# Two-layer conditional kernel on one core: the first batch's loads, turns and splits put in another order

## The reference

```python
# layer 0: x + x W0^T + b0 + coeff[b] * x (2 mask[b] - 1)
output = jnp.einsum('bsi,oi->bso', hidden_states, W) + b
sign = (2 * mask - 1).astype(hidden_states.dtype)
diff = jnp.einsum('bsi,bio->bso', hidden_states, sign)
x = x + output + diff * coeff[:, None, None]
# layer 1: y + y W1^T + b1 + (y A^T) B^T, A and B gathered by ids[b]
result = jnp.einsum('bsd,od->bso', x, base_weight) + base_bias
h = jnp.einsum('bsd,brd->bsr', x, lora_A_w[adapter_ids])
x = x + result + jnp.einsum('bsr,bor->bso', h, lora_B_w[adapter_ids])
```

## Time and profile before

| | |
|---|---|
| median of three runs | 433.26 us |
| the profiled execution, its time | 435.75 us |
| its span | 434.1 us |
| TensorE busy | 409.7 us (94%) |
| VectorE, ScalarE, GpSimd busy | 287.1, 184.6, 24.0 us |
| mean granted clock of TensorE | 0.978 of full speed |
| HBM read, written | 51.39 MB, 8.39 MB |

### The profile page before, as it was taken

The page is one execution under the profiler, slowest core; times in us unless marked ns, Lnnn a source line. Parts: engine busy times, 40 slices in busy tenths (PEclk is TensorE's granted clock), DMA queues, the critical chain, the costliest instruction groups (busy, mean ns, idle before and its releaser), DMA issues.

```text
span 434.1 us, 5456 instructions
## 1 busy us (share of the span) xinstructions
PE 409.7 (94%) x2049; PEld 342.3 (79%) x2049; DVE 287.1 (66%) x336; ACT 184.6 (43%) x288; POOL 24.0 (6%) x47
## 2 busy tenths in 40 slices
PE   3579998978999999999999999999999999999996
PEld 3568886757888888888888888888888888888884
DVE  0475658676688666776588767776678667866512
ACT  2264555454334533363343434444245433453312
POOL 4325401000000000000000000000000000000000
PEclk9788999899999999999999999999999999999999
DMA  6996796416943399309931595319921894237002
GB/s 224 253 333 195 207 211 179 86 48 151 249 125 94 108 193 222 97 1 233 237 100 50 131 240 150 98 74 209 236 64 36 196 241 120 61 110 169 2 0 97
DMA packets 90845, 63.28 MB, mean 146 GB/s; under 512 B 3515, under 2 KB 84419, under 8 KB 90820
## 3 DMA queue, kind: packets, MB, share of 16 engines
q1 hardware_dynamic: 89588, 59.28, 55.3%
q0 software_dynamic: 1232, 3.67, 2.7%
HBM read 51.39 MB, written 8.39 MB: 138 GB/s over the span
## 4 chain that ended last, share of the span: by engine, by line
PE 88%; DVE 6%; ACT 2%; DMA 2%; issue 1%; SPq 1%; ACTq 0%; DVEq 0%
PE ps L625 27%; PE ps L627 13%; PE ps L652 13%; PE ps L651 13%; PE ps L653 13%; PE ps L635 3%; PE ps L611 3%; PE ps L663 2%; DMA cs<-in_condB_coeff_dram 2%; DVE wm L488 1%; DVE wlo L495 1%; ACT whi L350 1%; DVE w1lo L460 1%; DVE xhl L471 1%; DVE xt L465 0%
## 5 line engine op out<-in xcount | busy, mean ns | idle before, releaser
L625 PE MATMUL ps<-xhl,whi 128*128 128x512 f32 x512 | 187.8, 405 | 2.0 <-DVE wlo L495 1.2
L627 PE MATMUL ps<-xhl,wlo 128*128 128x256 f32 x512 | 145.1, 283 | 0.0
L495 DVE SCALAR_TENSOR_TENSOR wlo<-wm,cs_minus,whi 128x1024 fp32r<-128x1024 f32 x64 | 83.0, 1296 | 53.2 <-ACT whi L350 52.8
L625 PEld LDWEIGHTS ps<-xhl,whi 128*128 128x128 f32 x512 | 97.7, 191 | 25.1 <-DVE wlo L495 1.5
L350 ACT ACTIVATE whi<-wm,cs_minus 128x1024 fp32r<-128x1024 f32 x64 | 73.7, 1151 | 81.7 <-DVE wm L488 80.5
L651 PE MATMUL ps<-w1hi,yhl 128*128 128x512 f32 x256 | 102.0, 398 | 0.0
L652 PE MATMUL ps<-w1lo,yhl 128*128 128x512 f32 x256 | 100.7, 394 | 0.0
L653 PE MATMUL ps<-w1hi,yhl 128*128 128x512 f32 x256 | 100.5, 393 | 0.0
L627 PEld LDWEIGHTS ps<-xhl,wlo 128*128 128x128 f32 x512 | 98.1, 192 | 2.5
L488 DVE SCALAR_TENSOR_TENSOR wm<-wm,cs_twice,w0t 128x1024 f32<-128x1024 int32 x64 | 81.8, 1278 | 11.7 <-ACT w0t L331 11.5
L652 PEld LDWEIGHTS ps<-w1lo,yhl 128*128 128x128 f32 x256 | 48.5, 189 | 10.7
(11 more groups left out here) (50 smaller groups left out, 178.7 us busy)
## 6 DMA issues: line engine op xcount, KB each, us to landing
wm<-in_mask_Bx4096x_ik_dram SPq DMA_DIRECT2D x64, 512.0 KB, 5.8
out_dram<-zst SPq DMA_DIRECT2D x32, 256.0 KB, 2.5
xraw<-in_x_dram SPq DMA_DIRECT2D x28, 256.0 KB, 7.4
w1raw<-_L_cond_base_weight_dram SPq DMA_DIRECT2D x8, 512.0 KB, 6.5
bt<-bhl SPq DMA_DIRECT2D x48, 64.0 KB, 2.9
w0raw<-in_L_cond_W_dram POOLq DMA_DIRECT2D x5, 512.0 KB, 6.7
w0raw<-in_L_cond_W_dram SPq DMA_DIRECT2D x3, 512.0 KB, 9.2
xrows<-in_x_dram SPq DMA_DIRECT2D x2, 512.0 KB, 7.0
```

The source lines that it names most:

```text
L495: nc.vector.scalar_tensor_tensor(wlo[:, s, :, :], wm[:, n % MS, :].rearrange("p (k o) -> p k o", k=KT), cs_minus[:, b:b + 1], whi[:, s, :, ...
L625: nc.tensor.matmul(ps[:, bank, :], whi[:, s, k, :], xhl[:, b % 2, k, :], start=(k == 0), stop=False, skip_group_check=True)
L627: op = nc.tensor.matmul(ps[:, bank, 0:S], wlo[:, s, k, :], xhl[:, b % 2, k, 0:S], start=False, stop=(k == KT - 1), skip_group_check=True)
```

## The change

Only batch 0 (and, in later batches, which half of x is turned first) changes. TensorE's, ScalarE's, VectorE's, GpSimd's and Sync's lists all move:

- the units get other banks: two banks for turning, 5 and 7; layer 0's product of steps 0 to 7 uses bank 4 alone, later ones 5 and 4 in turn;
- w0's chunk n+1 (not n+2) is turned in step n, so the weights are made one step ahead in batch 0, and VectorE catches up to two steps in step 7;
- A is turned inside step 1, B in step 4 instead of step 6; `adapter_h(0)` moves into step 2;
- the next x is turned by VectorE in the fourth and seventh step (n = 3 and 6), second half first;
- w0's chunks 3 to 7 go to Sync's list; four small loads go to ScalarE's queue; GpSimd issues A in pieces of 2, 4 and 2 around its first additions, B in two pieces of 4, and it splits the bias (`b1hi`, `b1lo`) that ScalarE and VectorE split before.

```diff
-    Z0, L1B, HB, TB = 0, 4, 6, 7
-    units = [("w0", 0, 0, 0), ("w0", 0, 1, 1), ("x", 0, 0, 4), ("x", 0, 1, 5), ("x", 1, 0, 6), ("x", 1, 1, 7),
-             ("w0", 1, 0, 2), ("w0", 1, 1, 3), ("w0", 2, 0, 0), ("w0", 2, 1, 1),
-             ("a", 0, 0, 2), ("a", 0, 1, 3), ("w1", 0, 0, TB), ("w1", 0, 1, HB)]
+    Z0, L1B, HB, TB = 0, 4, 6, (5, 7)
+    units = [("w0", 0, 0, 0), ("w0", 0, 1, 1), ("x", 0, 0, 2), ("x", 1, 0, 3), ("x", 0, 1, 6), ("x", 1, 1, 7),
+             ("w0", 1, 0, 0), ("w0", 1, 1, 1), ("w1", 0, 0, 2), ("w1", 0, 1, 3)]
     for n in range(1, KT):
...
+        if n + 1 < KT:
+            units += [("w0", n + 1, h, TB[h]) for h in range(2)]
+        if n == 4:
+            units += [("b", 0, h, TB[h]) for h in range(2)]
+        for h in range(2):
+            units.append(("w1", n, h, TB[h]))
+            if n == 1:
+                units.append(("a", 0, h, TB[h]))
...
+    def l1_bank(n):
+        return L1B if n < KT else L1B + (n + 1) % 2
...
@@ sync
...
             load_w1(1)
+            load_w0(3)
             load_mask(3)
...
             for n in range(NS):
+                if n + 4 < KT:
+                    load_w0(n + 4)
...
+                if n == 1:
+                    load_x(1)
                 if n == 3:
                     move_bias()
-                if n == 7:
+                if n == 5:
                     load_bt(0)
@@ gpsimd
             pool.wait_ge(ident_set, 2)
+            pool.wait_ge(ids_in, 16)
+            load_a(range(0, 2))
             eye_w0(0)
-            load_a()
+            load_a(range(2, 6))
             eye_w0(1)
+            load_a(range(6, NB))
             eye_w1(0)
-            load_w0(3)
             eye_w0(2)
-            load_w0(4)
             eye_w1(1)
-            load_w0(5)
             eye_w0(3)
-            load_w0(6)
+            load_b(range(0, 4))
             eye_w0(4)
             eye_w1(2)
+            load_b(range(4, NB))
             eye_w0(5)
-            load_b()
-            load_w0(7)
+            pool.wait_ge(b1_in, 16)
+            nc.gpsimd.tensor_copy(b1hi[:, :], b1raw[:, :]).then_inc(bias_hi, 1)
+            pool.wait_ge(bias_hi, 1)
+            nc.gpsimd.tensor_tensor(b1lo[:, :], b1raw[:, :], b1hi[:, :].bitcast(F32), ALU.subtract).then_inc(bias_lo, 1)
             eye_w1(3)
-            eye_w0(6)
@@ scalar
...
+            act.dma_start(cs[:, :], coeff.rearrange("(e b) -> e b", e=1).to_broadcast([P, NB])).then_inc(coeff_in, 16)
+            act.dma_start(b0row[:, :], b0.rearrange("(c p) -> c p", p=P)).then_inc(b0_in, 16)
+            act.dma_start(id_row[:, :], ids.rearrange("(e b) -> e b", e=1)).then_inc(ids_in, 16)
+            act.dma_start(b1raw[:, :], b1.rearrange("(e o) -> e o", e=1)).then_inc(b1_in, 16)
...
+                if n == 7:
+                    rows_hi(1, 0)
+                    chunk_hi(8)
+                half_y(n)
+                if n < 7:
+                    chunk_hi(n + 1)
                 y_parts_hi(n)
+                for h in range(2):
+                    split_hi("w1", n, h)
+                    if n == 1:
+                        split_hi("a", 0, h)
+                if n == 7:
+                    chunk_hi(9)
@@ tensor, layer1
+                    if n == 0:
+                        pe.wait_ge(b0_moved, 1)
+                    elif n < KT:
+                        pe.wait_ge(y_made, n)
+                    else:
+                        pe.wait_ge(y_made, n - 1)
+                    if n == KT:
+                        pe.wait_ge(parts_lo, parted(number["w1", KT - 1, 0]))
+                    if c == 0 and b > 0:
+                        pe.wait_ge(x_lo, x_split(b, 0))
```

More of the change, by code:

```diff
@@ L249, in _ @@
                     load_bt(b)
-                if c == 2 and b + 1 < NB:
+                if c == 3 and 0 < b < NB - 1:
                     load_x(b + 1)
@@ L270, in eye_w1, with load_a @@
                 nc.gpsimd.tensor_tensor(diag, diag, ident[:, :], ALU.add).then_inc(w1_eyed, 1)
[L272 to L278, removed]
-                for e in range(NB):
+            def load_a(adapters):
+                for e in adapters:
                     name = pool.value_load(id_row[0:1, e:e + 1], min_val=0, max_val=NL - 1)
@@ L524, in _ @@
             make_w(0)
-            first_rows_lo(0, 0)
             chunk_lo(0)
-            first_rows_lo(0, 1)
-            first_rows_lo(1, 0)
-            first_rows_lo(1, 1)
-            dve.wait_ge(b0_turned, 1)
-            nc.vector.tensor_copy(b0col[:, :], ps[:, TB, 0:KT]).then_inc(b0_moved, 1)
+            for g in range(2):
+                for st in range(ST):
+                    first_rows_lo(st, g)
             make_w(1)
@@ L584, in turn_unit @@
                 before = [v for v in range(u) if units[v][3] == bank]
-                if u == number["w1", 0, 0]:
-                    pe.wait_ge(b0_moved, 1)
                 if before and units[before[-1]][0] == "x":
-                    pe.wait_ge(x_lo, 4)
+                    pe.wait_ge(x_lo, first_split(*units[before[-1]][1:3]))
                 elif before and units[before[-1]][0] == "w0":
@@ L615, in layer1 @@
                 b, c = divmod(n, KT)
-                bank = L1B + n % 2
+                bank = l1_bank(n)
                 s = n % WS
@@ L703, in _ @@
                     pe.wait_ge(consts_set, 3)
-                    pe.wait_ge(w0_copied, copied(number["w0", 2, 1]))
+                    pe.wait_ge(w0_copied, copied(number["w0", 1, 1]))
+                    pe.wait_ge(parts_lo, parted(number["w1", 0, 1]))
+                    pe.wait_ge(y_lo, 1)
+                    layer2(0, 0, 0)
+                    turn_unit("w1", 1, 0)
+                    layer2(0, 0, 1)
+                    turn_unit("a", 0, 0)
+                    layer2(0, 1, 0)
+                    turn_unit("w1", 1, 1)
+                    turn_unit("a", 0, 1)
+                    layer2(0, 1, 1)
+                    continue
                 if m < KT:
```

180 lines of the change are left out of this document (84 added, 96 removed).

## The result

The changed kernel takes **442.54 us** (median of four runs, 441.93 to 443.49), the kernel before 433.44 us beside it on the same chip: a ratio of **1.020, 95% interval 1.014 to 1.026**. It is slower, by some 9 us (whether by more than 2% the interval leaves open), where 435.5 us (431.0 to 439.5) was forecast.

A forecast was written before the change was run, and what follows sets the result against it. TensorE, busy without a gap from 100.60 us, bounds the kernel, so only step 9's start can move: +0.55 us, plus 1.7 for half clock, gives +2.25 on the median of 433.26, so 435.5 us, range 431.0 to 439.5.

The forecast's parts named there:

- Start: Up to step 1: numbers land in 3.0 us, first addition at 8.3, step 1 at 25.8 against 27.60, gain 1.8 us.
- A in step 1: TensorE waits 2.5 and 1.7 us before A's two halves; step 2 at 38.1 against 40.18, 0.4 for half clock.
- Steps 2 to 4: TensorE waits for GpSimd's additions to w1's chunks 2 and 3, done at 44.35 and 53.25; step 5 at 65.7.
- Steps 5 to 9: End of batch 0: step 7 at 81.7, step 8 at 90.65 held by VectorE, step 9 at 101.15.
- The wait before `finish`: In step 8, TensorE waits 3.7 us for VectorE's chain where 1.78 stood before.
- the 1.7 us that I added for it: Behind step 9: half clock after the last wait adds 1.7 us, half of 3.4.
- The sum: Step 9 later by 0.55 us plus 1.7 for half clock: +2.25 us, profiled execution 438.0, median 435.5.
- (A): Whole kernel: the sum holds, all waits from the lists' order and measured durations, 435.5 us, slower; chance 0.38.
- (B): Step 0, step 2 and last wait: TensorE's clock does not fall, 432.6 us, no change; chance 0.2.
- (C): Steps 3 and 4: GpSimd not late, B loads at 0.55 us each, 432.1, or 430.5 with (B) in part; chance 0.2.
- (D): Numbers land at 7.2, b1lo takes 3.6, or half clock follows the wait before step 1: 437 to 440; chance 0.22.

The follow-up runs named there:

- e5: Changed kernel with the four small loads issued from Sync's queue again, ids first, coefficients behind x: 442.30 us, ratio 1.0205.
- e4: Changed kernel with GpSimd's descriptor space at 1536 bytes instead of 1024, h's parts put over `abraw`: 437.69 us, ratio 1.0104.
- e10: Changed kernel with e3's order, A in bank 6, batch 0's end reordered, bias and w1 chunk 2's addition earlier, descriptor space 1024 bytes: 432.84 us, ratio 0.997.
- e1: Changed kernel with GpSimd's addition to w1's chunk 3 moved ahead of the second piece of B loads: 438.49 us, ratio 1.0107.
- e3: Changed kernel with the addition to w0's chunk 0 again ahead of all A loads: 440.72 us, ratio 1.0168.
- e12: e10 with descriptor space of 1536 bytes, h's parts over `abraw`, and w1 chunk 3's addition ahead of b1hi: 424.25 us, ratio 0.978.

## Why the prediction was right or wrong

Starts of the steps, as forecast and as measured:

| step | 0 | 1 | 2 | 3 | 4 | 5 | 7 | 8 | 9 |
|---|---|---|---|---|---|---|---|---|---|
| forecast | 16.5 | 25.8 | 38.1 | 47.7 | **56.2** | 65.7 | 81.7 | 90.65 | 101.15 |
| measured | 17.38 | 25.81 | 38.27 | 47.00 | **62.53** | 71.73 | 87.83 | 96.82 | 107.13 |

- **Start: right by luck.** The addition came at 8.97 (forecast 8.3; its terms add to 8.2), and step 1 at 25.81 as forecast, but only because two errors of 0.9, in step 0's start (17.38 for 16.5) and in its length (8.43 for 9.3), cancel. The numbers took 7.29 - 1.5 - 1.91 = 3.9 us to land (1.5 is the prediction's time from a number to its first load; GpSimd's read of `id_row` starts at 5.7), against the 3.0 taken; first in Sync's own queue (e5) they took 3.67 - 1.5 - 0.86 = 1.3. By the Trainium skill (DMA: Bandwidth & Descriptors, section Queues, rings and completion order) each DMA engine takes its queue rows in turn. The prediction's estimate of 2 us from that rule was too low for the numbers behind two other loads on ScalarE's queue.
- **A in step 1: right.** Waits of 2.5 and 1.7 were forecast, 2.31 and 1.41 came. Half clock behind them, taken at 0.4 us, did not come in this execution (1.00 from 36 to 48 us); in e4's and e5's it did (0.76 and 0.72), and step 2 started there at 39.75 and 40.85.
- **Steps 2 to 4: this step failed.** "Next, four more loads, an addition, b1hi, b1lo, then the addition to w1's chunk 3: ... 8.9, done at 53.25." It was done at 56.80, 12.9 after the one to chunk 2 (43.88). Of the 4.0 more, 3.3 are the pause before the eighth load (e4, e10), 0.8 is b1lo: 3.20 for 2.4, inside its bounds of 1.2 to 3.6. The prediction had no term for a pause. Nor had it one for the clock here: behind the 5.16 us wait TensorE ran 5.6 us at half clock (0.50), 2.6 us more to step 4 than the 3.0 forecast (in e4 the same stretch, at full clock, took 57.00 - 54.01 = 3.0). In all 6.3 us at step 4, and the error at step 9 is still 6.0. The row that spoke for a pause was in the trace of before. GpSimd's timeline of that kernel, the first three, the seventh and the eighth B load:

```profile
37.80 1.66 POOL L289 DMA_DIRECT2D abraw<-in_L_cond_lora_B_w_dram  x3
...
43.93 0.53 POOL L289 DMA_DIRECT2D abraw<-in_L_cond_lora_B_w_dram  x1 [0.72 <-issue]
46.65 0.53 POOL L289 DMA_DIRECT2D abraw<-in_L_cond_lora_B_w_dram  x1 [2.19 <-issue]
```

The last gap is 2.72 us, the four before it are 1.25, the first two 0.55. I took the spacing of the fifth and sixth for all eight. TensorE did not wait for it in that kernel, and the change took that cover away.
- **Steps 5 to 9: right in length.** 9.2, 16.1 for two steps, 9.0 and 10.3 us against 9.5, 16.0, 8.95 and 10.5. The wait before `finish` was forecast at 3.7 and was 1.73, though the end came on time: half clock fell from 96.8 to 99.9 us (0.51), behind the 2.18 us wait for step 8, and made TensorE arrive later at a wait that VectorE and ScalarE set anyway. So half clock came where it cost nothing, and the 1.7 us that I added for it behind step 9 did not come (1.00 from 107.1 on). In e1's and e3's executions it did: 0.79 and 0.90 over step 9, which took 7.14 and 6.31 us instead of 5.75.
- **The sum, and its base.** 438.0 was forecast for the profiled execution, 442.15 came: 4.2 us, which is (within 0.2) the 6.0 at step 9 less the 1.7. That it came out slower is in part luck: of the +2.25 forecast, the 1.7 did not come in this execution and the other 0.55 is less than a measurement tells, while the pause and the half clock in step 3, of which the sum knew nothing, brought the 6. The other 2.9 of the 7.0 us between 435.5 and 442.54 come from carrying the profiled execution's distance from the median over: the one before lay 2.5 above its median, the one after 0.4 below. The executions of before that ran beside the experiments fit this: the nine at a granted clock of 1.00 take 431.1 to 433.5 us, those at 0.978 take 435.1 to 436.6, so its half clock comes and goes, and the profiled one had all of it. The changed kernel's profiled execution was at 0.985, and its four runs lie within 1.6 us.
- **Rivals.** (A) had the right place, TensorE waiting in step 3 for GpSimd's list, but not the cause of its length: it held that all waits come from the lists' order and measured durations, and the pause and the half clock come from neither. (B), the clock does not fall, is excluded (0.50 in step 3). (C)'s forecast did not come: the addition to w1's chunk 2 was done at 43.88, not before 43, and the loads ahead of it followed each other by 1.15 us. But its mechanism exists. Behind additions, loads do follow each other by 0.55: three in 1.66 us in the kernel before (37.80), three in 1.67 us in e4 (45.75), behind an addition that took 1.46. In the changed kernel the first four stand behind an idle GpSimd, and behind the two short additions at 43.00 only one load was ready (43.81). (D) "longer still", 437 to 440: of its three, the numbers took 3.9 us and not 7.2, no half clock followed the wait before step 1, and b1lo took 3.20, between the 2.4 of the sum and its 3.6. The pause was in none of the cases.

## What to carry to other kernels

Before transfers of an engine are put closer together or on the waited-for path, read each one's gap in the old trace, the last as well as the first: a gap that grows without a releaser can be a limit that the old order covered. And before a wait is taken out of a list, find which other wait ends last in the same stretch: three cuts ahead of the pause were worth 1.8, 0.8 and, with a wait of its own, 0.2 us while it stood. With the larger space, the end of batch 0 put right and the bias split out of the way, the same order runs 9 us below the kernel before (e12). How much of that is the cuts' own wasn't taken apart. Where an idle stretch of TensorE brings half clock, price it by what stands behind it: 2.6 us in step 3, where TensorE was last, and, as far as the forecast of that step came true without it, nothing in step 8, where VectorE was.
